# A fused token, attention and expert kernel: one padded load of the feature weights, and the last two image octets inside the attention steps

## What is computed

```
tok = jnp.concatenate([main, xl, xr, yu, yd], axis=-1)
h = (tok - mu) * jax.lax.rsqrt(var + EPS) * ln_g + ln_b
h = jnp.concatenate([h, txt], axis=1)
h = h + _L0_attn_ref(_layernorm(h, axis=-1), Wq, Wkv, Wo, bo)
h = h + _L0_ffn_ref(_layernorm(h, axis=-1), gate_w, expert_bias, shared_gate_up, shared_down, expert_gate_up, expert_down)
```

## Time and profile before

| | us |
|---|---|
| median of 3 runs | 872.37 |
| lowest, highest | 871.62, 872.62 |
| the profiled execution, as a whole | 871.01 |
| its span, first to last instruction | 869.0 |

### The profile page before, as it was taken

How to read it: one execution, slowest core, us unless ns; L and a number is a source line. 1 busy time by engine, 2 the same in 40 slices (tenths; PEclk the granted TensorE clock), 3 DMA queues, 4 the chain that set the end, 5 groups by cost and what they waited for, 6 DMA issues and landing times.

```text
span 869.0 us, 19935 instructions
## 1 busy us (share of the span) xinstructions
PE 667.5 (77%) x6114; PEld 550.3 (63%) x6114; DVE 604.5 (70%) x2034; ACT 446.2 (51%) x1058; POOL 553.3 (64%) x695
## 2 busy tenths in 40 slices
PE   3845899989999899998999868898788787875000
PEld 2633788877788787877887745676567566664000
DVE  1686789989889898997988955465545555544184
ACT  0643888877778777876787721343333223231000
POOL 3354124776756767667686777277777777777463
PEclk9976999999889999998999958899998989998555
DMA  9810000100101001010010114676666666661496
GB/s 288 240 37 20 2 3 10 35 31 29 34 22 34 31 28 34 29 31 27 29 35 30 35 41 154 195 217 184 193 172 188 180 178 184 177 183 46 123 370 190
DMA packets 66540, 88.38 MB, mean 102 GB/s; under 512 B 14118, under 2 KB 59055, under 8 KB 66282
## 3 DMA queue, kind: packets, MB, share of 16 engines
q1 hardware_dynamic: 30212, 35.74, 14.5%
q10 hardware_dynamic: 23680, 28.06, 10.8%
q0 software_dynamic: 12544, 23.31, 8.1%
HBM read 56.46 MB, written 33.01 MB: 103 GB/s over the span
## 4 chain that ended last, share of the span: by engine, by line
DVE 25%; issue 18%; PE 17%; POOL 16%; DMA 11%; ACT 2%; SPq 1%; POOLq 0%; DVEq 0%; ACTq 0%
POOL expert_rows L551 8%; DMA expert_rows<-yb,dst_i 7%; POOL dispatched L538 4%; DVE mx L1173 4%; PE bank L611 3%; DVE s L1178 3%; DMA x2t<-expert_rows 3%; PE bank L712 3%; PE bank L745 2%; DVE o L1208 2%; DVE v L1175 2%; PE bank L698 2%; PE bank L795 2%; DVE st L1187 1%; DVE vr L1214 1%
## 5 line engine op out<-in xcount | busy, mean ns | idle before, releaser
L551 POOL DMA_INDIRECT expert_rows<-yb,dst_i x200 | 195.5, 978 | 75.0 <-issue 53.1
L538 POOL DMA_INDIRECT dispatched<-pay,sloti x192 | 204.2, 1063 | 55.2 <-issue 49.6
L795 PE MATMUL bank<-xe,kt 128*128 128x256 f32 x400 | 109.6, 399 | 0.0
L1291 DVE TENSOR_TENSOR yb<-bank,gd 128x256 f32<-128x256 f32 x100 | 42.2, 422 | 95.8 <-DMA expert_rows<-yb,dst_i 93.4
L953 ACT ACTIVATE xe<-bank 128x256 f32<-128x256 f32 x100 | 38.3, 383 | 137.2 <-PE bank L783 133.0
L804 PE MATMUL bank<-kt,hide 128*128 128x128 f32 x400 | 69.4, 298 | 47.9 <-DVE hide L1281 47.7
L804 PEld LDWEIGHTS bank<-kt,hide 128*128 128x128 f32 x400 | 59.1, 201 | 71.4 <-DVE hide L1281 68.3
L611 PE MATMUL bank<-xt,wqkv 128*128 128x452 f32 x384 | 101.9, 397 | 1.2 <-DVE xt L1192 0.7
L508 POOL TENSOR_SCALAR ve<-mv 113x1 f32<-113x1 f32 x64 | 15.1, 236 | 96.2 <-DVE mv L1198 95.9
L795 PEld LDWEIGHTS bank<-xe,kt 128*128 128x128 f32 x400 | 72.3, 201 | 6.1
L611 PEld LDWEIGHTS bank<-xt,wqkv 128*128 128x128 f32 x384 | 69.6, 197 | 6.8 <-DVE xt L1192 0.9
(11 more groups left out here) (165 smaller groups left out, 1701.4 us busy)
## 6 DMA issues: line engine op xcount, KB each, us to landing
kt<-in_w_ffn ACTq DMA_DIRECT2D x100, 192.0 KB, 2.6
xs_all<-dispatched SPq DMA_DIRECT2D x100, 140.0 KB, 2.6
x2t<-expert_rows SPq DMA_DIRECT2D x16, 672.0 KB
out_h<-h ACTq DMA_DIRECT2D x16, 224.0 KB
x2t<-in_x ACTq DMA_DIRECT2D x4, 864.0 KB, 7.3
x2t<-in_x SPq DMA_DIRECT2D x4, 864.0 KB, 7.2
expert_rows<-yb,dst_i POOLq DMA_INDIRECT x200, 2.8
dispatched<-pay,sloti POOLq DMA_INDIRECT x192, 2.4
```

What stands on the lines that cost most here:

```text
L538: pool.indirect_dma_start(out=xs_dram[:, :], out_offset=bass.IndirectOffsetOnAxis(ap=sloti[:, q % (PAYS // GRP), b % GRP, c:c + 1], axis=0 ...
L551: pool.indirect_dma_start(out=y_dram[:, :], out_offset=bass.IndirectOffsetOnAxis(ap=dst_i[:, slot, j:j + 1], axis=0), in_=yb[slot % RW][:, ...
L795: m = nc.tensor.matmul(bank[3 - i][:, j * TR:(j + 1) * TR], w_ex[slot][:, j * F:(j + 1) * F], xe[1 - i][:, :], start=True, stop=True)
```

## The change

Three things are done.

The feature weights are put together on the host as one array with its zeros, `w_feat`, and loaded into `wz` by a single transfer of 3,072 bytes for each partition; GpSimd's memset of `wz` and the SP queue's wait for it go.

VectorE's four splits of the attention weights stand behind `centred(0)` (now in two functions, `token_stats` and `centred`).

The image stage's loops end two octets earlier on VectorE and GpSimd. What is left goes into the first steps. On VectorE: `token_stats` of octets 6 and 7 at k = 0 and 2 of octet -1, `centred` at k = 1 and 3, `first_stats` of octets 4 and 5 at k = 4 and 5, and those of octets 6 and 7 at k = 2 and 4 of octet 0. The clearing of bank 5 moves to k = 5. GpSimd's `patch_scale`, `patch_shift` and `first_eps` and ScalarE's `scaled` follow. TensorE's program keeps its order; its waits for `tok_g` and `pt_zero` stand before the first scores instead of before the first step.

```diff
@@ sync
-            sp.wait_ge(S["wz_zero"], 1)
-
-            sp.dma_start(wz[:, :, 0:64], w_main).then_inc(S["wz_in"], 16)
-            sp.dma_start(wz[64:128, :, 64:80], w_sx[0:64]).then_inc(S["wz_in"], 16)
-            sp.dma_start(wz[0:64, :, 80:96], w_sx[64:128]).then_inc(S["wz_in"], 16)
-            sp.dma_start(wz[:, 3:6, 96:112], w_sy[:, 0:3]).then_inc(S["wz_in"], 16)
-            sp.dma_start(wz[:, 0:3, 112:128], w_sy[:, 3:6]).then_inc(S["wz_in"], 16)
+            sp.dma_start(wz[:, :, :], w_feat).then_inc(S["wz_in"], 16)
@@ gpsimd
-            nc.gpsimd.memset(wz[:, :, :], 0.0).then_inc(S["wz_zero"], 1)
...
-            for o in range(NOCT):
+            for o in range(NOCT - 2):
...
-            patch_shift(NOCT - 1, (NOCT - 1) % 2)
-            first_eps(NOCT - 3)
+            patch_shift(NOCT - 3, (NOCT - 3) % 2)
+            first_eps(NOCT - 5)
+
+            def image_rest(o, k):
+
+                if o == -1 and k in (1, 3):
+                    patch_scale(NOCT - 2 + k // 2, k // 2)
+                elif o == -1 and k in (4, 5):
+                    first_eps(NOCT - 8 + k)
+                    patch_shift(NOCT - 6 + k, k % 2)
+                elif o == 0 and k in (2, 4):
+                    first_eps(NOCT - 3 + k // 2)
@@ tensor
-            pe.wait_ge(S["wz_in"], 80)
+            pe.wait_ge(S["wz_in"], 16)
...
-            pe.wait_ge(S["tok_g"], NOCT)
...
-            pe.wait_ge(S["pt_zero"], 5)
...
                     after(pe, "s_copied", n + 1, 0)
+                    if n == -1:
+                        pe.wait_ge(S["tok_g"], NOCT)
+                        pe.wait_ge(S["pt_zero"], 5)
@@ scalar
-            for o in range(NOCT + 2):
-                if o < NOCT:
-                    shifts(o)
-                if 1 <= o <= NOCT:
+            for o in range(NOCT):
+                shifts(o)
+                if o >= 1:
                     biased(o - 1)
                 if o >= 2:
                     scaled(o - 2)
-            act.wait_ge(S["pt_zero"], 5)
+            biased(NOCT - 1)
...
+                if o == -1 and k in (3, 4):
+                    scaled(NOCT - 5 + k)
@@ vector
-            for o in range(NOCT):
+            for o in range(NOCT - 2):
+                token_stats(o)
                 centred(o)
+                if o == 0:
+                    dve.wait_ge(S["attn_in"], 96)
+                    nc.vector.tensor_copy(wqkv[:, 0, :], wqkv_stage).then_inc(S["w_split"], 1)
...
+            def image_rest(o, k):
+
+                if o == -1 and k in (0, 2):
+                    token_stats(NOCT - 2 + k // 2)
+                elif o == -1 and k in (1, 3):
+                    centred(NOCT - 2 + k // 2)
+                elif o == -1 and k in (4, 5):
+                    first_stats(NOCT - 8 + k, k % 2)
+                    if k == 5:
+                        nc.vector.memset(bank[5][:, :], 0.0).then_inc(S["pt_zero"], 1)
+                elif o == 0 and k in (2, 4):
+                    first_stats(NOCT - 3 + k // 2, k // 2 - 1)
...
-                if isinstance(o, int) and o == -1 and k in (4, 5):
-
-                    first_stats(NOCT - 2 if k == 4 else NOCT - 1, 0 if k == 4 else 1)
...
                 routing(o, k, 0)
+                image_rest(o, k)
                 if ok(n - 2):
```

More of the change, by code:

```diff
@@ L1011, in centred @@
                 m.then_inc(S["tok_stat"], 1)
+            def centred(o):
+                i, tok = o % 2, bank[4 + o % 2]
                 after(dve, "tok_stat", o)
```

38 lines of the change are left out of this document (20 added, 18 removed).

## The result

| | us |
|---|---|
| kernel before, median of 14 runs | 871.89 (867.60 to 873.24) |
| changed kernel, median of 14 runs | 866.03 (860.99 to 869.76) |
| ratio after / before, with its 95% interval | 0.9945 [0.9926, 0.9964] |
| profiled execution of the changed kernel, as a whole | 866.14 |
| its span | 864.2 |

The change makes the kernel faster by 0.55%, that is 4.8 us with an interval of 3.1 to 6.5; the two medians are 5.9 apart, which lies within it. The forecast was 10.3. The sign and the mechanism were right; about half of the gain didn't come. The median lies within the range of 857.0 to 868.5, outside the forecast's own of 859.5 to 865.

What follows compares the result with a forecast made beforehand. No engine bounds the whole run; early on TensorE waits for weight loads, then image 6, and VectorE bounds from 47.47 us. Terms -7.6 + 2.3 + 0.7 - 10.7 + 0.9 + 4.15 = -10.3 us gave 862.1, range 857.0 to 868.5.

Steps and rivals of the forecast that it cites:

- the forecast's own: Range of the main forecast of 862.1 us, 859.5 to 865, given a chance of 0.60.
- issued at 31.1, landed 5.76 later at 36.8: Load of octet 6's image: issued 5.3 us earlier, landing at 36.8; called the least certain of the times.
- the transfer of image 6 doesn't come earlier: Rival: transfers ahead in the SP queue hold image 6 until 42.1, losing the start's gain; 866.7 us, chance 0.12.
- from octet 1 on everything would be as before: Sign: from octet 1 of the steps on, all unchanged and 10.3 us earlier; a growing difference would make the prediction wrong.
- The start: TensorE's first matmul at 6.2 instead of 13.78, a gain of 7.6 us; bounds of the start 5.4 and 12.9.
- The clock at image 6: TensorE's 12 projections behind the longer gap before image 6 lose 0.7 us, between 0 and 1.0.
- The splits: VectorE's weight splits behind the first centring run from 21.5 to 25.2 and cost 2.3 us of the gain.
- Two octets fewer: Image stage before the steps: two VectorE periods of 5.12 us and the 0.48 us bank memset leave, gaining 10.7 us.
- the same work in the first eight steps: Moved image work inside the steps before octet 0 costs net 0.9 us; scores start 14.4 us earlier, at 71.0.
- The late statistics: Input statistics of octets 6 and 7 in steps 2 and 4 of octet 0 cost 4.15 us, bounds 0 and 5.0.
- The rival that they would be hidden: Rival: steps 2 and 4 of octet 0 have room, so the 4.15 us go; 857.9 us, chance 0.11.
- The rival of the clock: Rival: gaps of 2 us in octet 0 drop TensorE's clock; three steps' worth lost gives 877 us, slower's chance 0.05.

Runs made afterwards that it cites:

- after_again: The changed kernel run once more with no edit; 864.50 us, ratio to the kernel before 0.9909.
- no_stats67: The changed kernel without the input statistics of octets 6 and 7, those of octet 5 standing in; ratio to the kernel before 0.9843.
- spread: The changed kernel with the statistics of octets 6 and 7 in small pieces where VectorE waits; 859.87 us, ratio to the kernel before 0.9848.
- load_only: The kernel before with only the single load of the padded weight array; ratio to the kernel before 1.0011.
- load_splits: The kernel before with the single weight load and VectorE's four splits behind `centred(0)`; ratio to the kernel before 1.0021.
- spread_text: The changed kernel with late statistics in small pieces and the second text half moved ahead of octet 4's rows; 858.74 us, ratio to before 0.9830.
- before_again: The kernel before run once more with no edit; 872.21 us.
- text_behind3: The changed kernel with only the second text half moved behind the token rows of octet 3; 861.55 us, ratio to the kernel before 0.9899.
- rest_only: The changed kernel with the five weight loads, memset and splits as before, so only the moved octets; ratio to the kernel before 0.9960.
- text_late: The changed kernel with the second text half and `w_sh` loaded behind the image of octet 7; ratio to the kernel before 0.9950.

## Where the prediction was right, and where it failed

**The step that failed** is "issued at 31.1, landed 5.76 later at 36.8". The issue came at 31.36. The landing came at 39.46, 8.1 us behind the issue (8.2 to 9.3 in after_again, no_stats67, spread, load_only and load_splits). The 5.76 was measured in the kernel before, in a place where the text ahead of it in its queue was nearly in, and I carried it over to a place where it wasn't. Windows of 5 us with the share of the transfer engines second from last and GB/s last, first of before:

```profile
30.00:35.00 5.00, 5.00 (x27) 4.03 (x25) 3.08 (x16) 4.49 (x15) 2.50 (x3) 1.00 0.91 178
35.00:40.00 5.00, 3.60 (x18) 2.49 (x16) 3.58 (x22) 4.36 (x13) 2.50 (x3) 1.00 0.67 207
40.00:45.00 5.00, 2.87 (x8) 2.14 (x9) 4.53 (x28) 1.72 (x5) 2.75 (x5) 0.80 0.72 226
```

then of the changed kernel:

```profile
25.00:30.00 5.00, 3.82 (x18) 2.97 (x19) 3.02 (x14) 4.07 (x13) 2.50 (x3) 1.00 1.09 327
30.00:35.00 5.00, 4.12 (x20) 2.96 (x18) 2.22 (x12) 3.87 (x11) 2.50 (x3) 1.00 0.92 180
35.00:40.00 5.00, 0.54 (x1) 0.50 (x2) 2.70 (x19) 0.93 (x3) 0.00 (x0) 0.81 0.97 302
40.00:45.00 5.00, 5.00 (x12) 3.46 (x11) 4.54 (x29) 1.28 (x4) 3.67 (x5) 0.50 0.08 32
```

Now the transfer engines are full from 5 us to 40 us (0.87 to 1.19 in each window), and when image 6 has landed they are done. Summed over the windows from 0, 11.6 MB had been moved by 40 us; before, 10.6 MB by 40 us and 11.7 by 45. The image stage has become bound by its transfers, which an earlier issue doesn't lessen (the bytes alone don't measure them: a full window moved between 180 and 402 GB/s). In spread_text, where the text stands elsewhere, the shares from 25 to 35 us are 0.39 and 0.59, and image 6 lands 5.7 us after its issue.

What the load waits for can be read more closely from `w_sh`, the last load behind the text. Its row in the kernel before, with the us from its issue at 24.05 to its landing:

```profile
w_sh<-in_w_ffn SPq DMA_DIRECT2D x1, 192.0 KB, 13.3
```

It landed at 37.35 before and at 35.94 in the changed kernel, 1.0 and 4.6 us behind the issue of image 6. So this last load had moved by only 1.4 us, and image 6 landed behind it both times. after_again and before_again show the same: image 6 is issued 3.1 us apart (32.00 and 35.10), `w_sh` lands at 38.19 and 38.08, and image 6 is used at 41.28 and 41.04. The forecast called this landing the least certain time, said that the text might not be gone by then, and gave that no price; the landing of `w_sh` in the trace of before, 1 us behind the issue that was to come 5.3 us earlier, would have given it one.

**A second transfer that the forecast left out** is held by the same text. The rows of octet 0 stand behind it and ahead of image 6 in the queue. In all nine executions with the text ahead VectorE waited for them and had them 0.7 to 1.3 us behind the landing of `w_sh`, whether this came 2.3 or 8.1 us behind their issue. Before, that was 3.5 us after their issue at 34.47:

```profile
38.01 1.64 DVE L995 BATCH_NORM_STATS2 st<-h 113x6 f32<-113x128 f32 x8 [1.25 <-DMA h<-xs_all]
```

Now it took 7.6 us, from 29.47 to 37.10. Between that start and the tokens of octet 4 VectorE has 7.8 us of work with no gap over 0.4 (37.37 to 45.19 in spread, 39.14 to 46.95 in after_again, 34.42 to 42.21 in text_behind3). In the changed kernel this chain ends at 44.9 and TensorE's, by image 6, at 45.83; in spread and after_again the rows are the later of the two, and image 6 costs nothing beyond them. So with image 6 at 36.8 as forecast, the statistics of octet 4 would still have started at 44.9 and not at 42.9. That is 2.0 of the 2.9 us by which these statistics were late; TensorE's chain by image 6 adds the last 0.9. The rival "the transfer of image 6 doesn't come earlier" (866.7) was nearest in its size, and named one of the two transfers: of 5.0 us of earlier issue 2.7 arrived for the image, and 0.9 for the rows. That its time fits so well is luck: it gave the start no gain, where 1.6 us were left of it at the statistics of octet 4, and it had no fall of the clock, which took 1.4.

**Its other steps**, with the forecast first:

| step | forecast | measured |
|---|---|---|
| first matmul | 6.2 | 6.61, waiting for image 0 |
| tokens of octet 1 behind the splits | 25.2 | 25.48 |
| image 6 issued | 31.1 | 31.36 |
| image 6 used | 36.8 | 39.46 |
| its 12 projections | 4.87 + 0.7 | 5.89 |
| statistics of octet 4 | 42.9 | 45.83 |
| octet 4 to the first `xn` | 10.8 | 10.75 |
| first `xn` to the scores | 17.3 | 17.35 |
| steps 2 and 4 of octet 0 | 4.15 | 5.63, of which 1.4 clock |
| lead behind them | 10.3 | 5.90 |

The differences are the sum of the miss: 2.9 at the statistics of octet 4 (along TensorE's chain, which ended last: landing 2.3, issue 0.3, clock 0.3), and 1.5 in steps 2 and 4. That is 4.4, and takes 10.3 to 5.9. Another us goes between the 5th step and the end of the span, which is no more than before_again wanders. The forecast's sign that from octet 1 on everything would be as before failed as well: the lead moved between 3.0 and 6.9 us there.

**The start.** The cost bounds (5.4 to 12.9) held and the value was well taken. By the sentence on the rings served in turn (the Trainium skill, DMA: Bandwidth & Descriptors, Queues, rings and completion order) the weights would land with the first image, at about 6. The trace agrees: 6.2, and TensorE's wait ends with image 0 at 6.61. The issue at 0.80 instead of 1.55 gives the wait for the zeros 0.75 us of that gain; for the rest one load and its larger pieces came together, and no run separates them.

**The clock at image 6.** The term was 0.7 between 0 and 1.0. The changed kernel had all of it, 5.89 us, and so did spread_text (5.98); the others lie on the side of before: 4.56, 4.87, 4.87, 4.68 and 4.55 us (load_only, load_splits, after_again, no_stats67, spread). The length of the gap doesn't decide it, since 5.45, 3.88, 3.88, 5.87 and 5.43 us gave the short ones and 5.34 and 3.32 the long. Windows of half a us show what does. The clock goes down to its lower level (0.50) at each of these gaps, but at another place: in after and spread_text it goes down over a us ahead of the first projection and is back 5.5 us into them; in load_only and spread it goes down just before them and is back after 2.8; in load_splits it is still whole at their start, goes down half a us later and is back after 4.3. So the bound of 0 was as good as that of 1.0, and a single value was more than one trace can carry. By the sentence on the clock behind waits on transfers (the Trainium skill, TensorE: Matmul & The Clock Gate, HAM oscillation) each of these bursts would start at half rate; five of the seven do, and after_again and load_splits follow within 0.2 and 0.6 us. That this makes the upper end each time was my reading, and two of seven traces have it.

**The splits.** Right in their place and time. In either place they are over before transfers that are later anyway, and the result is the same to 0.1 us (load_only against load_splits); no run has them off this path altogether.

**Two octets fewer, and the same work in the first eight steps.** Both terms held to 0.1 us. The waits for ScalarE's copy take up the token statistics as worked out.

**The late statistics.** 4.15 forecast, 4.2 measured in the two executions without a clock fall. The rival that they would be hidden fell with no_stats67, where leaving them out brings it all back, and spread shows that it would have been true of pieces of 0.5 to 0.9 us put ahead of the reciprocal. The rival of the clock was right in kind and small: one fall, not three, for 1.4 us. "From 85 to 90 us TensorE was idle for over a quarter of the time and the clock stayed whole" spoke of short gaps (0.85 us at most in that stretch); that of step 4 is 2.1 us in one piece.

What stays open is what decides whether the clock falls after such a gap, and why the changed kernel's own runs lie between 861 and 870 us: the landing (39.5 to 41.3) and the clock in step 4 move its trace by 1 to 2 us each, the clock from octet 1 on by up to 3, and I have not shown that they explain all of that. Nor is it shown why the leads of 2.3 us in load_only and load_splits don't reach their times.

## What to carry to other kernels

A time from issue to landing holds only for the queue and the load in which it was measured; ahead of an earlier issue, look when the transfers that stand before it in its queue land, and at the share of the transfer engines there, since where these are full the order of the queue counts and the time of the issue hardly does. Work that is moved into the slack of a full stage has to be cut to about the size of one slack and put where the engine waits: 2.5 us of statistics in one piece cost 2.1 us, and in pieces of 0.5 us ahead of the reciprocal nothing. And follow each engine back from the place where two chains meet: here a small transfer of rows, which no step of the forecast named, held VectorE as much as the large image held TensorE.

## What the runs showed of the hardware

- An image load of 864 KB took 5.2 to 6.0 us from issue to use where `w_sh`, the last weight load ahead of it in its queue, landed before the issue or at most 3 us behind it (before, before_again, rest_only, text_behind3, spread_text) or wasn't ahead (text_late), and 8.1 to 9.3 where it landed 4.4 to 6.2 us behind the issue (after, after_again, load_only, load_splits, no_stats67, spread). The transfer engines' share between issue and use was 0.57 to 0.91 in the first and 0.84 to 0.96 in the second, so the share alone doesn't tell them apart.
- Two transfers of 72 KB with the text ahead took 3.5 to 5.9 us from issue to use in before, before_again and rest_only, and 7.4 to 9.0 in the six executions with an issue 3 to 6 us earlier; they were used 0.7 to 1.3 us behind the landing of `w_sh` in all nine executions.
- Behind a gap of 2.1 us in a full stretch TensorE's granted clock stayed whole in two executions and fell to between 0.51 and 0.64 for two windows of 2 us in three, the first windows after the gap. It cost 1.4 us.
- At the gap before image 6 TensorE's clock went down to 0.50 in all ten executions with a gap of 3.3 to 5.9 us, and in neither of the two with 0.2 and 0.4 us (text_behind3, text_late; 3.18 us for the 12 projections). Behind the longer gaps they took 4.55 to 4.87 us or 5.9 to 6.0, by where the low stretch began. Kernels that are alike up to there, with nearly the same gap, gave either: 5.34 us of gap and 5.89 in after, 5.43 and 4.55 in spread.
